# The mask product of a windowed attention kernel, laid by eight narrow products in place of two wide ones

## What is computed

```python
def local_attention(q, k, v):          # w = 32, heads 16, head dim 64
    ...
    mask = (it < jb) | (it > jb + w) | (jb == -1)
    sim = jnp.einsum('bhwie,bhwje->bhwij', bq, bk2) * QK_SCALE
    sim = jnp.where(mask, -jnp.finfo(sim.dtype).max, sim)
    attn = jax.nn.softmax(sim, -1)
    out = jnp.einsum('bhwij,bhwje->bhwie', attn, bv2)
```

## Time and profile before

| | us |
|---|---|
| three timed runs, median (lowest to highest) | 3814.31 (3814.22 to 3814.42) |
| profiled execution, its span from first to last instruction | 3806.1 |
| PE busy | 3546.5 (93%) |
| DVE busy | 3233.6 (85%) |
| ACT busy | 2526.1 (66%) |
| POOL busy | 1558.0 (41%) |

### The profile page before, as it was taken

One profiled execution on the slowest core, in us unless ns is written; L12 is line 12 of the kernel. 1 busy time (PEld: TensorE's weight loads), 2 busy tenths in 40 slices (PEclk: granted clock), 3 DMA queues, 4 the chain that ended last, 5 costly groups with the idle time before them and its releaser, 6 DMA issues. The chain is left out here.

```text
span 3806.1 us, 123350 instructions
## 1 busy us (share of the span) xinstructions
PE 3546.5 (93%) x51360; PEld 2001.1 (53%) x51360; DVE 3233.6 (85%) x3696; ACT 2526.1 (66%) x3409; POOL 1558.0 (41%) x926
## 2 busy tenths in 40 slices
PE   5999879899999999999999999999999999999997
PEld 2333245555555555555555555555555555555554
DVE  7999778788888888888888888888888889888895
ACT  4888757667666666666766667667666666666764
POOL 4333144344434444434444434344444434444341
PEclk7999989999999999999999999999999999999999
DMA  2000011111121111121111111111211111211112
GB/s 69 2 1 1 23 44 34 28 27 34 29 61 34 27 34 28 37 58 27 34 28 34 50 38 34 28 29 38 55 34 29 27 40 27 62 29 27 37 30 62
DMA packets 60833, 130.63 MB, mean 34 GB/s; under 512 B 16004, under 2 KB 31880, under 8 KB 60424
## 3 DMA queue, kind: packets, MB, share of 16 engines
q1 hardware_dynamic: 60424, 124.06, 13.4%
HBM read 23.58 MB, written 4.19 MB: 7 GB/s over the span
## 5 line engine op out<-in xcount | busy, mean ns | idle before, releaser
L798 POOL TENSOR_TENSOR half_sq<-sq 128x1024 f32<-128x1024 f32 x192 | 500.9, 2609 | 1541.9 <-ACT sq L933 1531.9
L1072 PE MATMUL slot<-w_qkv,xs 128*128 (+1 forms) x2304 | 1102.7, 608 | 25.6 <-issue 17.3
L803 POOL TENSOR_TENSOR cosq<-cosq,sinq 128x1024 f32<-128x1024 f32 x384 | 902.2, 2366 | 368.7 <-DVE sinq L843 368.7
L933 ACT ACTIVATE sq<-slot 128x1024 f32<-128x1024 f32 x384 | 392.0, 1021 | 405.3 <-PE slot L1072 405.3
L1072 PEld LDWEIGHTS slot<-w_qkv,xs 128*128 128x128 f32 x2304 | 411.2, 192 | 432.2 <-issue 423.5
L841 DVE TENSOR_TENSOR cosq<-slot,table 128x1024 f32<-128x1024 f32 x384 | 467.7, 1218 | 143.4 <-ACT sq L933 133.1
L869 DVE TENSOR_TENSOR qk<-cosq,ry 128x1024 f32<-128x1024 f32 x384 | 517.8, 1359 | 11.6 <-ACT ry L990 9.5
L843 DVE TENSOR_TENSOR sinq<-slot,table 128x1024 f32<-128x1024 f32 x384 | 465.8, 1213 | 0.0
L1023 PEld LDWEIGHTS slot<-ident,qk 128*128 128x128 f32 x3072 | 349.5, 141 | 215.0 <-issue 125.3
L1023 PE MATMUL slot<-ident,qk 128*128 128x128 f32 x3072 | 396.1, 275 | 36.4 <-DVE qk L869 32.2
L1053 PE MATMUL slot<-vb,probT 128*32 128x130 f32 x6144 | 327.7, 280 | 16.9 <-issue 10.6
(11 more groups left out here) (123 smaller groups left out, 4940.6 us busy)
## 6 DMA issues: line engine op xcount, KB each, us to landing
vb<-va SPq DMA_DIRECT2D x720, 130.0 KB, 2.3
w_qkv<-in_w_qkv SPq DMA_DIRECT2D x21, 512.0 KB, 5.3
w_o<-in_w_o SPq DMA_DIRECT2D x6, 512.0 KB
w<-in_w SPq DMA_DIRECT2D x6, 342.0 KB
res<-in_x SPq DMA_DIRECT2D x4, 512.0 KB, 5.3
out<-w_qkv SPq DMA_DIRECT2D x8, 256.0 KB, 3.2
kept<-res SPq DMA_DIRECT2D x1, 1536.0 KB, 6.2
w<-in_w SPq DMA_DIRECT2D x6, 171.0 KB
```

Of the source, the lines that this page charges most:

```text
L798: nc.gpsimd.tensor_tensor(half_sq[:, :, :], squares[:, :, 0, :], squares[:, :, 1, :], ALU.add).then_inc(S["folded"], 1)
L803: nc.gpsimd.tensor_tensor(cosq[:, side], cosq[:, side], sinq[:, side], ALU.add).then_inc(S["qk"[side] + "_added"], 1)
L933: nc.scalar.activation(sq[:, "qk".index(name)].rearrange("p h d -> p (h d)"), flat(name, n), ACT.Square).then_inc(S[name + "_squared"], 1)
L1072: last = nc.tensor.matmul(slot(kind, n)[:, i, :], xs[:, n * P:(n + 1) * P], w_qkv[:, (0 if layer is None else layer) % 2, "qkv".index(kind ...
```

## The change

The two mask products of a stage `s` become eight: one for each group g of 32 output rows and each half r. The weights are a unit matrix of 32 columns, `unit16`, in place of the 64x64 one twice; the mask streams as before, 512 columns for each product. A `passed(pe)` is put ahead of the stage.

```diff
-        self.pair16 = sb("pair16", [P, 2, DH], BF16)
+        self.unit16 = sb("unit16", [P, WIN], BF16)
...
-                nc.scalar.copy(early.pair16[rows, :, :], ident[rows, None, rows].broadcast_to([DH, 2, DH])).then_inc(
+                nc.scalar.copy(early.unit16[rows, :], ident[rows, DH * r:DH * r + WIN]).then_inc(
                     early.S["const_ready"], 1)
...
             def scores(t):
-                for r in range(2):
-                    rows = slice(DH * r, DH * r + DH)
-
-                    nc.tensor.matmul(slot("s", t)[:, r, :], pair16[rows, :, :].rearrange("p a n -> p (a n)"),
-                                     mask[rows, 0 if t == 0 else 1, :],
-                                     start=True, stop=False, skip_group_check=True)
+                for g in range(4):
+                    for r in range(2):
+                        rows = slice(DH * r, DH * r + DH)
+
+                        nc.tensor.matmul(slot("s", t)[32 * g:32 * g + 32, r, :], unit16[rows, :],
+                                         mask[rows, 0 if t == 0 else 1, :],
+                                         start=True, stop=False, skip_group_check=True)
...
                 elif kind == "s":
                     wait(pe, "qT_read", unit, n)
                     wait(pe, "kT_read", unit, n)
+                    passed(pe)
                     last = scores(n)
```

More of the change, by code:

```diff
@@ L649, in windowed_stack @@
         table = sb("table", [P, TPB, 4, DH])
-        pair16 = early.pair16
+        unit16 = early.unit16
         mask = early.mask
```

## The result

The changed kernel takes 3823.62 us (median of 8 runs, 3815.09 to 3835.43) against 3814.26 us for the kernel before (8 runs, 3807.95 to 3818.75): a ratio of 1.0029, 95% interval 1.0015 to 1.0043. It is slower by 0.29%. The profiled execution of the changed kernel has a span of 3816.9 us, 10.8 more than before's 3806.1.

The account below looks back on a forecast made before the run. PE, busy for 93% of the span, was taken as the bound. Terms -13.0 + 4.5 + 6.5 = -2.0 us on 3806.1, -4 with the one-in-nine chance of 18 us; plus 8.2 us to timed runs: 3810 us, range 3790 to 3829.

Parts of the forecast that it names:

- Removed: one change of shape: Between mask and scores, the array shape no longer changes from 64*128 to 64*32: 0.09 us saved a stage.
- Added: six more streams: In the mask, eight products on separate array pieces run together, so the extra streams were taken to cost 0.
- The rival of eight serial masks: In the mask, the eight products do not run together: 0.66 us x 144 = +95 us, 3896 us; chance 0.03.
- Added: 13 instructions: In the dense scores stage, instruction delivery leaves a gain between 0.03 and 0.2 us a stage, taken as 0.09.
- The semaphore increment: Ahead of s0 and s3, handing over after the wait may add 0.1 us; taken as equal with an earlier delivery start.
- The term of -13.0: Stages s0, s1 and s2 each gain 0.09 us in 48 units, -13.0 us; s3 saves nothing because of slack.
- The padding: Ahead of the loop, 200 no-ops in place of 139, 0.074 us each: +4.5 us, paid once.
- The pauses by "issue": In the loop, moved ends of 256-instruction blocks lengthen PE's pauses by 0.6 us a pass, x 11: +6.5 us (+3 to +10).
- one chance in nine and 18 us: Second unit's s3: the pause of about 5.13 us in five passes might fall to 1.60, giving back 18 us.
- slower by the block ends: Rival: ends in s3 or s2 in three of four units cost more, +15 us, 3829 us; chance 0.20.
- the two cases: Whole kernel: balance, most likely 3810 us, chance 0.37, and slower through the block ends, 3829 us, chance 0.20.

Follow-up runs that it names:

- experiment 2: The kernel before with only the semaphore increment `passed(pe)` added ahead of the scores: 3811.75 us, ratio 0.9990.
- experiments 3 and 4: Changed kernel and kernel before, each with filling no-ops moved to the start of TensorE's program: 3802.19 us (0.9965) and 3805.20 us (0.9974).
- place 0: Both kernels with the loop's head on a block end, no no-ops ahead of the loop: changed kernel 3812.32 us, kernel before 3804.43 us.
- place 32: Both kernels with the loop's head 32 instructions behind a block end, no no-ops ahead of it: changed kernel 3777.96 us, kernel before 3753.66 us.
- place 192: Both kernels with the loop's head 192 instructions behind a block end, no no-ops ahead of it: changed kernel 3855.68 us, kernel before 3814.44 us.
- experiments 5 to 16: Both kernels with the loop's head 0, 32, 64, 84, 128 or 192 instructions behind a block end: changed 3777.96 to 3859.80 us, before 3753.66 to 3814.44 us.

## Why the prediction was wrong, point by point

*Removed: one change of shape. Added: six more streams.* Right. The first score comes at 0.23 us, and eight masks make a union of 0.41 us. The rival of eight serial masks is out.

*Added: 13 instructions.* A stage without a pause takes 1.62 us in s1 where it took 1.73 (1.81 in the stage of the earlier trace rows), a gain of 0.12 us, in the forecast's 0.03 to 0.2. *The semaphore increment*, taken as equal, costs 0.11 us ahead of s3 and 0.09 ahead of s0: experiment 2 shows it alone. By the medians of the stages over the stack's units s1 and s2 gain 0.12, s0 0.13 less 0.09, and s3's gain goes into the longer wait at kT0: 0.27 us a unit, 48 of them 13 us. PE's busy time says nearly the same: 19.3 us less, and 4.6 and 4.2 us of it back in the waits of L1031, which leaves 10.5. The term of -13.0 stood, in part by luck: the gain was 0.12 and not 0.09, and the increment that was put at nothing took the difference.

*The padding.* 200 no-ops, 12.06 for 7.72 us of idle: +4.3 for the 4.5 forecast.

*The pauses by "issue".* This is the step that failed, by its size: +6.5 us, where the profile has 17 to 19 (10.8 less 4.3, and the 10.5 to 13 saved), as the 10.0 us of "issue" and the 9.5 us of qk above also say.

First, I counted the eleven passes alone. The ends also moved in the units that are written out ahead of the loop, a term that I put at nothing without a reason. It is 4.6 us in the profile, 5.7 with what the masks saved there.

Second, in the loop the pauses came to some 13.5 us (1.6, and the 12 saved in its 44 units) and not to 6.5, and they fell otherwise than I counted. By the stretches from one stage to the next, in the eleven passes: the second unit from s3 to kT0 got 27.4 us shorter, since its pause, there in eleven passes before and 4.6 us or more in five of them, is left in three passes and long in one. I had left it where it was, and gave a shrinking of it one chance in nine and 18 us. The fourth unit from s3 to kT0 got 20.3 us longer, where I had 6.7. The stretches from s2 on in the third and fourth unit got 12.5 and 10.1 us longer, where I had 5.9 and 12.1. Two more pairs of traces with the same ends in the loop (experiments 3 and 4, and place 0) have 24 us shorter for the first, 18 to 23 longer for the second, 12 and 9 longer for the others. So the sum for the loop is as near as it is by large errors of both signs.

Why did the count fail? I gave each end a pause from the time that its block took, and the second table shows that for s2 it hangs on whether the end lies past a certain place in the stage. s2 is interrupted in the first unit in part, and in the second, third and fourth in every pass, by 1.0 to 1.2 us each in the mean of the stage's length, where I had 0.54 and 1.1 for two of them. The third unit's s3, given 1.60 us, is free in ten passes of eleven, while the fourth's has 2.0 to 2.5 in ten. The chance of 0.20 for "slower by the block ends" named this mechanism, with 1.6 us for each of four ends and no wait to replace. The measured 3823.6 lies between the two cases.

The Trainium skill (Runtime: NRT & Kernel Launch, Instruction fetch mechanics) has the crossing of a block mostly hidden. In these traces most crossings are hidden, and those of a dense stage are not: from 560 to 3690 us the pauses by "issue" sum to between 32 us (kernel before, place 32) and 140 us (changed kernel, place 192).

*What stays open.* That the loss at an end comes from a late fetch is read from the packets; that the place of the ends moves the time is shown by experiments 5 to 16. Why the changed kernel is behind at every place is not settled; its four units have their ends in s2 only 21 instructions apart, so that they fare alike, and six places are few. Two narrow masks and `passed` have the loss at place 32 (+36 to +48 us), `passed` with the old masks has none at place 0 (-3 us), and eight wide masks with `passed` are near the changed kernel in both places. The step `passed` goes with fetches that are late at an earlier place in s2, and the six products lengthen the stage behind it; how much each takes, and whether narrow masks alone would have it, no run tells. Neither the changed kernel without the step `passed` nor the kernel before with it at place 32 was tried. What sets the moment at which a block is asked for is not known either.

## What to carry to other kernels

Before a change of a few instructions in a long dense loop is judged, move the block ends: the same two kernels differ by +0.15% to +1.8% with the loop's head at six places, and two lines of alignment (the kernel before, head at 32, fill at the start) give 3753.7 us, 1.5% under it as it was, more than any form of the mask. The ends move ahead of a loop too, and short stretches there can hold most of a loss. A gain read from a stage's timeline counts only if the stage isn't fed late: ask where the next block's fetch begins, what the pause covers, and what else is on the DMA queues at that moment. No-ops that fill up to a boundary cost 0.074 us each where the engine is the bound, and no trace shows a cost of them at the start, where it waits.

## What the runs showed of the hardware

- A pause by "issue" at a block end in a stage of scores lasts until 2.2 to 3.3 us after its fetch packet starts, in every kernel, mostly 2.3 to 2.7. The packet itself is short, within 0.1 us; its start is what varies.
- In s2 the fetch comes either 2.6 to 9.7 us ahead of the stage or with it, and some 20 instructions turn the one into the other: in the kernel before an end at 198 was early in ten passes of eleven, one at 219 in none.
- Where the weights of the next layer are loaded (287 GB/s, engines 89% busy) a late fetch in s3 begins 3.7 to 5.3 us after the stage's first product and not 0.9 to 1.7, and the pause is 4.6 to 6.1 us and not 1.5 to 2.5. Behind a pause of 5.13 us the granted clock was 0.57 for 5 us, behind one of 1.60 us 1.00.
- Eight products of 64 x 32 pieces with 512 columns make a union of 0.41 us, where two of 64 x 128 make 0.39. The change of array shape between them and the scores was 0.09 us.
- A semaphore increment ahead of a stage that has to wait makes the wait 0.09 to 0.11 us longer, though nobody waits for the increment.
